# Differential attention: another order of SyncE's transfers in a turn, and the normed output transposed one unit earlier into the other half of a PSUM bank

## The chip, the core and the metric

The kernel runs on one core of a Trainium2 chip. Its engines work side by side, each through its own list of instructions: TensorE (PE, with its weight loads as PEld), VectorE (DVE), ScalarE (ACT), GpSimd (POOL) and SyncE (SP), which here only issues DMAs. They wait for each other through semaphores. The metric is the time of one execution on the device in microseconds; less is better.

## The reference

The whole reference is a stack of two layers on x of shape 16 x 256 x 128: a mixture of experts, a differential attention, the mixture of experts again, a quantized feed-forward, a linear attention and the feed-forward once more. The change touches the differential attention alone:

```
q = (x @ Wq.T + bq)   16 heads, two maps of 8 numbers each; k alike; v: 16 heads of 8
q1, q2, k1, k2 = rope(...)                       # on both maps
a1 = softmax(causal(q1 @ k1.T * 8**-0.5))        # 256 x 256 for each head
a2 = softmax(causal(q2 @ k2.T * 8**-0.5))
out = (a1 - lam * a2) @ v
out = out * rsqrt(mean(out * out) + 1e-6) * head_norm_w * 0.8
return out @ Wo.T + bo                           # added to x
```

The input of the attention is the layernorm of x, and x is first completed with the fetched outputs of the experts.

## The kernel before

`diff_attention` takes the 16 sequences (batches, `NB = 16`) through a pipeline that is four batches deep. The loop `turns` runs 19 turns on every engine. In turn `it`, batch A = `it` is projected, rotated and packed; B = `it - 1` gets its scores and the maxima of their rows (`scores` on PE, `maxima` on DVE); C = `it - 2` gets its transposed scores, its exponentials on ACT and the product with v; D = `it - 3` is divided, normed, multiplied by Wo and added to x. For each engine a turn is a list of 24 units (`STEPS = 24`, variable `u`), written out by hand: what belongs to unit 13 is issued after what belongs to unit 12, and so on. There is no scheduler; the order on each engine is the order in the code.

What the change touches:

- **SyncE's turn** (`turn` under `@block.sync`). It has helpers, each a wait or two and four DMAs (one for `yg`): `block_queries(b, half)` (L1775) copies half of the packed, transposed queries `qT` into the stacked tile `q_block`; `pair_keys` (L1785) does that for the keys; `peaks(b, half)` (L1793) writes the transposed row maxima into a row of `qT`; `spread_values` (L1766) copies `v_raw` into `v_new`; the fetch (L1811) brings 256 KB of expert outputs for a later batch from HBM into `yg`. SyncE waits in order, so a helper that is not ready holds everything behind it.
- **Who needs them.** `scores(B, 0)`, the first score product of the next turn, waits on PE for `q_block_in[0]` (its first instruction is the mask product L2363). `scores_T(C, 0)` (L2384, L2388) stands ahead of it and needs `peaks` and `pair_keys` of the same half. The second halves are needed at unit 12. `v_new` is read by POOL's `keep_v` at unit 3 of the next turn, and `yg` by POOL's `weigh_fetched` at unit 1.
- **The bank of the values.** `m_ps[:, 0]` is one PSUM bank of 512 fp32 columns. At unit 12 PE writes the projected values of A into its columns 0 to 255; at unit 13 ACT copies them to `v_raw` (L1985). At unit 14 PE transposes the normed output of D (`on`, made by DVE at unit 12, L2304; it shares its memory with `osq`, and the profile prints it as `diff_osq`) into the same columns (L2549), and therefore waits for `v_taken`; ACT copies the result to `onT` (L1991). At unit 15 PE transposes the packed queries into this bank (L2573), for which `onT` must have been copied, and ACT's `keep_peaks` (L1948) at unit 15 is what SyncE's `peaks` waits for.

Of the kernel before, what the change touches and what calls it, by code (L numbers as in the profile page):

```python
# [12 lines left out]
ACT = mybir.ActivationFunctionType  # L13
AX = mybir.AxisListType

P = 128
# [1496 lines left out]
def diff_attention(nc, tag, x, ident, neghalf, made, later, ew, routed):  # L1513
# [16 lines left out]
    S = 2 * P  # L1530
    NB = (x.shape[1] - TG) // 2
# [28 lines left out]
    with ExitStack() as ctx:  # L1560
# [54 lines left out]
        on = osq  # L1615
        onT = nm.sb("onT", [P, S], F32)
# [4 lines left out]
        m_ps = nm.ps("m_ps", [P, 2, 512], F32)  # L1621
        m16 = [m_ps[:, i].bitcast(F16) for i in range(2)]

        if ew:
            yg = nm.sb("yg", [P, 2, 2, P], F32)
# [21 lines left out]
        fetched = nm.sem("fetched")  # L1647
        fetch_weighed = nm.sem("fetch_weighed")
        fetch_added = nm.sem("fetch_added")
# [20 lines left out]
        v_taken = nm.sem("v_taken")  # L1670
# [19 lines left out]
        o_weighted = nm.sem("o_weighted")  # L1690
# [6 lines left out]
        onT_in_psum = nm.sem("onT_in_psum")  # L1697
        onT_ready = nm.sem("onT_ready")
# [53 lines left out]
        @block.sync  # L1752
        def _(sp):
            sp.wait_ge(packs_ready, 7)

            def chunks(half):
                return slice(CH // 2 * half, CH // 2 * half + CH // 2)

            def spread_values(b):

                sp.wait_ge(v_taken, b + 1)
                if b >= 1:
                    sp.wait_ge(v_ready, b)
                for i in range(2):
                    for j in range(2):
                        sp.dma_start(v_new[KB * j:KB * j + KB, i::2], v_raw[KB * i:KB * i + KB]).then_inc(v_dup_in, 16)  # L1766

            def block_queries(b, half):

                sp.wait_ge(packT_ready, b * 4 + (4 if half else 1))  # L1770
                if b >= 1:
                    sp.wait_ge(s_ready, (b - 1) * STEPS + HALF * (half + 1))
                for r in range(4):
                    rows = slice(PACK * r, PACK * r + PACK)
                    sp.dma_start(q_block[rows, chunks(half), :, r], qT[rows, b % 3, chunks(half)].rearrange(  # L1775
                        "p c (i q) -> p c i q", q=QB)).then_inc(q_block_in[half], 16)

            def pair_keys(b, half):

                sp.wait_ge(packT_ready, b * 4 + 3)  # L1780
                if b >= 1:
                    sp.wait_ge(st_ready, (b - 1) * EXPS + EXP_HALF * (half + 1))
                for r in range(4):
                    rows = slice(PACK * r, PACK * r + PACK)
                    sp.dma_start(k_pair[rows, r // 2, chunks(half), :, r % 2], kT[rows, b % 2, chunks(half)].rearrange(  # L1785
                        "p c (i k) -> p c i k", k=KB)).then_inc(k_pair_in[half], 16)

            def peaks(b, half):

                sp.wait_ge(peakT_ready, b * 2 + half + 1)  # L1790
                for r in range(4):
                    row = PACK * r + USED - 1
                    sp.dma_start(qT[row:row + 1, b % 3, chunks(half)].rearrange("p c (i q) -> p (c i) q", q=QB),  # L1793
                                 peakT[half][:, QB * r:QB * r + QB].unsqueeze(1)).then_inc(peaks_in[half], 16)

            def turn(A, B, C, D, par):
                if B is not None:
                    block_queries(B, 1)
                if C is not None:
                    pair_keys(C, 1)  # L1800
                    peaks(C, 1)
                if B is not None:
                    pair_keys(B, 0)
                    peaks(B, 0)
                if A is not None:
                    spread_values(A)
                    block_queries(A, 0)
                    if ew and A + 2 < NB:
                        if A >= 1:
                            sp.wait_ge(fetch_added, A * 2)  # L1810
                        sp.dma_start(yg[:], ew.results[:, 2 * A + 4:2 * A + 6]).then_inc(fetched, 16)  # L1811

            turns(sp, turn)
            for half in range(2):
                sp.wait_ge(q_block_in[half], NB * 64)
                sp.wait_ge(k_pair_in[half], NB * 64)
                sp.wait_ge(peaks_in[half], NB * 64)
            sp.wait_ge(v_dup_in, NB * 64)
            if routed:
                for i in range(2):  # L1820
                    sp.wait_ge(scattered[i], len(range(i, routed - 1, 2)) * 2 * TG * 16)
# [99 lines left out]
        def _(a):  # L1921
# [28 lines left out]
            def turn(A, B, C, D, par):  # L1950
                norms, routes, places, sends = groups(D)
                for u in range(STEPS):
# [27 lines left out]
                    if A is not None:  # L1980
                        if u == 13:
                            a.wait_ge(v_in_psum, A + 1)
                            if B is not None:
                                a.wait_ge(v_dup_in, (B + 1) * 64)
                            nc.scalar.activation(v_raw[:].rearrange("p j h d -> p (j h d)"), m_ps[:, 0, 0:S], ACT.Copy).then_inc(v_taken, 1)  # L1985
                    if D is not None:
                        if u == 8:
                            guess_rms(D)
                        if u == 14:
                            a.wait_ge(onT_in_psum, D + 1)  # L1990
                            nc.scalar.activation(onT[:], m_ps[:, 0, 0:S], ACT.Copy).then_inc(onT_ready, 1)  # L1991
                    if B is not None and u == 15:
                        keep_peaks(B, 0)
                    if A is not None:
# [11 lines left out]
                        if u in (11, 12):  # L2006
                            j = u - 11
# [9 lines left out]
                        if u in (17, 18):  # L2017
                            j = u - 17
# [8 lines left out]
                        if u in (21, 22):  # L2027
                            j = u - 21
# [317 lines left out]
        def _(pe):  # L2346
# [110 lines left out]
            def turn(A, B, C, D, par):  # L2457
                norms, routes, places, sends = groups(D)
                for u in range(STEPS):
# [20 lines left out]
                    if u == 1 and A is not None:  # L2480
# [3 lines left out]
                        for j in range(2):  # L2484
                            last = nc.tensor.transpose(m_ps[:, 0, j * P:(j + 1) * P], xn[:, j], ident[:])
# [13 lines left out]
                    if u == 5 and D is not None:  # L2499
# [14 lines left out]
                        for j in range(2):  # L2514
                            for c in range(4):
                                at = (c % 2) * S + j * P
                                last = nc.tensor.transpose(m_ps[:, j, c * P:(c + 1) * P], oT[:, c // 2, at:at + P], ident[:])
                        last.then_inc(o_in_psum, 1)
                    if u == 7 and A is not None:
# [7 lines left out]
                        for j in range(2):  # L2527
                            for part in range(2):
                                last = project(m_ps[:, part, j * QK:(j + 1) * QK], j, slice(part * QK, (part + 1) * QK))
                        last.then_inc(qk_in_psum, 1)  # L2530
                    if u == 12 and A is not None:
                        pe.wait_ge(rope_taken, A * 2 + 2)
                        for j in range(2):
                            last = project(m_ps[:, 0, j * P:(j + 1) * P], j, slice(2 * QK, QKV))
                        last.then_inc(v_in_psum, 1)
                    if routes is not None and u == 13:
# [2 lines left out]
                            router_product(routes)  # L2539
                        else:  # L2540
                            ranks(routes)
                    if u == 14 and D is not None:
                        pe.wait_ge(on_ready, D + 1)
                        if A is not None:
                            pe.wait_ge(v_taken, A + 1)
                        else:
                            pe.wait_ge(o_weighted, D + 1)
                        for j in range(2):
                            last = nc.tensor.transpose(m_ps[:, 0, j * P:(j + 1) * P], on[:, j].rearrange("p h d -> p (h d)"), ident[:])  # L2549
                        last.then_inc(onT_in_psum, 1)  # L2550
                    if u == 15 and B is not None:
                        if routes is not None:
# [24 lines left out]
                    if u == 16 and D is not None:  # L2577
# [9 lines left out]
                        for j in range(2):  # L2587
                            out = m_ps[:, 1, j * P:(j + 1) * P]
                            nc.tensor.matmul(out, two_ones[:], wo_rows[:], start=True, stop=False)
                            last = nc.tensor.matmul(out, onT[:, j * P:(j + 1) * P], wo[:], start=False, stop=True)  # L2590
# [536 lines left out]
```

## Time and profile before

| | |
|---|---|
| median of 3 runs | 1248.44 us (1246.51 to 1251.01) |
| the profiled execution | 1243.69 us, its span 1241.9 us, so 1.8 us lie around the span |
| differential attention | about 239.9 to 779.9 us of the span |
| a full turn (first score product to the next turn's first) | 29 to 33 us |
| granted TensorE clock | 0.92 over the span, 0.95 in the attention |

The profile is that of one execution. A timeline row gives the start, the duration, the engine, the line of the code, the operation with the tile written and the tiles read, how many instructions were merged, and in square brackets how long the engine had been idle before it and what it had waited for. A window row gives busy time and number of instructions, then the granted clock as a share of 2.4 GHz, the DMA engines' busy share and GB/s. "SPq" is SyncE's queue; the duration there is that of issuing the transfers, not of moving the data.

### The profile page before, as it was taken

To read this page: it belongs to the slowest core of one execution; us is meant where nothing else is said; L and a number is where in the kernel's file an instruction comes from. 1 tells how busy PE (TensorE), PEld (TensorE's weight loads), DVE (VectorE), ACT (ScalarE), POOL (GpSimd) and SP (SyncE) were. 2 spreads that over 40 slices of the span, in tenths; PEclk is the share of its full clock that TensorE was granted. 3 is DMA by queue.
4 is the path that set the end of the run, shared out by engine and by line. 5 is a ranking of instruction groups with operands and counts; after the bars stand their busy time and mean duration, and the time that the engine had idled before them with its cause. 6 is when DMAs were issued, how large, how long until landed. Compare 5 with 4: busy or idle time off the path is not lost. (4 is left out here: it accounts for less than half of the span.)

```text
span 1241.9 us, 30962 instructions
## 1 busy us (share of the span) xinstructions
PE 989.9 (80%) x10944; PEld 731.5 (59%) x10976; DVE 859.7 (69%) x2352; ACT 660.6 (53%) x1247; POOL 654.9 (53%) x705
## 2 busy tenths in 40 slices
PE   3762999378888888788888887689993989999597
PEld 1531777145666666565666664578871855666476
DVE  7881887465667776767676765598876937877672
ACT  4730655435666666666656665346652644443163
POOL 5874677243333354544454433517772408888651
PEclk9875999688999999999989999689995989999899
DMA  8213431034433334433444331333314000000001
GB/s 241 80 48 98 116 110 66 34 45 60 54 54 53 56 57 62 58 59 54 61 62 62 51 63 28 110 112 104 99 57 141 3 1 2 1 1 2 1 26 44
DMA packets 273893, 75.52 MB, mean 61 GB/s; under 512 B 217040, under 2 KB 267504, under 8 KB 273360
## 3 DMA queue, kind: packets, MB, share of 16 engines
q1 hardware_dynamic: 264304, 52.51, 22.8%
q0 software_dynamic: 9440, 21.02, 4.9%
q8 instruction: 93, 1.52, 0.6%
q14 instruction: 56, 0.46, 0.1%
HBM read 28.08 MB, written 24.17 MB: 42 GB/s over the span
## 5 line engine op out<-in xcount | busy, mean ns | idle before, releaser
L2111 DVE TENSOR_REDUCE diff_peak<-diff_s_ps 128x2 f16<-128x384 f32 (+7 forms) x384 | 208.4, 558 | 141.1 <-PE diff_s_ps L2366 139.8
L1959 ACT ACTIVATE diff_prob<-diff_st_ps 128x512 f32<-128x512 f32 x320 | 187.1, 598 | 131.3 <-PE diff_st_ps L2388 130.1
L433 POOL DMA_INDIRECT exp_ys<-moe_y_sb,moe_dest x156 | 152.2, 975 | 87.0 <-ACT moe_y_sb L516 53.7
L2388 PE MATMUL diff_st_ps<-diff_qT,diff_k_pair 128*128 128x256 f16 (+3 forms) x1024 | 129.4, 240 | 3.5 <-issue 2.5
L2366 PE MATMUL diff_s_ps<-diff_kT,diff_q_block 128*128 128x32 f16 (+7 forms) x1024 | 130.4, 233 | 0.0
L2404 PE MATMUL diff_ot_ps<-diff_prob,diff_v 128*32 128x256 f32 (+3 forms) x2048 | 112.8, 317 | 0.5 <-ACT diff_prob L1959 0.5
L2363 PE MATMUL diff_s_ps<-diff_mask,diff_ident_bf 128*128 128x64 bf16 (+1 forms) x384 | 81.0, 211 | 39.6 <-DMA diff_q_block<-diff_qT 32.5
L509 ACT ACTIVATE moe_h_hi<-moe_h 128x512 f16<-128x512 f32 x94 | 59.2, 630 | 88.2 <-DVE moe_h L741 88.2
L2718 POOL TENSOR_TENSOR lin_y<-lin_state,lin_qT 128x512 f32<-128x512 f32 x64 | 81.1, 1268 | 15.5 <-DVE lin_state L2866 12.8
L2866 DVE TENSOR_TENSOR_SCAN lin_state<-lin_lam_ps,lin_kv 128x512 f32<-128x512 f32 x64 | 76.6, 1215 | 10.0 <-POOL lin_kv L2705 7.8
L2937 PEld LDWEIGHTS lin_o_ps<-last_lin_wo,lin_y 128*128 128x128 f32 x512 | 65.0, 191 | 26.6 <-POOL lin_y L2718 21.3
L503 ACT ACTIVATE moe_act<-moe_g_ps 128x512 f32<-128x512 f32 x94 | 55.7, 593 | 46.0 <-PE moe_g_ps L963 42.5
L416 POOL DMA_INDIRECT exp_xs<-moe_xh,exp_rows x64 | 66.7, 1042 | 23.8 <-issue 19.0
L2937 PE MATMUL lin_o_ps<-last_lin_wo,lin_y 128*128 128x128 f32 x512 | 70.3, 281 | 10.4 <-POOL lin_y L2718 10.4
L2363 PEld LDWEIGHTS diff_s_ps<-diff_mask,diff_ident_bf 128*128 128x128 bf16 x384 | 38.8, 101 | 61.8 <-issue 39.4
L741 DVE TENSOR_TENSOR moe_h<-moe_act,moe_u_ps 128x512 f32<-128x512 f32 x94 | 64.4, 685 | 15.4 <-PE moe_u_ps L963 14.4
L2388 PEld LDWEIGHTS diff_st_ps<-diff_qT,diff_k_pair 128*128 128x128 f16 x1024 | 70.6, 100 | 5.4
L736 DVE TENSOR_TENSOR moe_h_lo<-moe_h,moe_h_hi 128x512 f16<-128x512 f32 x94 | 65.0, 691 | 10.4 <-ACT moe_h_hi L509 10.0
L2404 PEld LDWEIGHTS diff_ot_ps<-diff_prob,diff_v 128*32 128x32 f32 x2048 | 53.2, 114 | 29.2 <-issue 14.2
L2384 PE MATMUL diff_st_ps<-diff_mask_T,diff_ident_bf 128*128 128x128 bf16 (+1 forms) x288 | 67.9, 236 | 2.0 <-ACT diff_prob L1959 1.8
L2366 PEld LDWEIGHTS diff_s_ps<-diff_kT,diff_q_block 128*128 128x128 f16 x1024 | 66.5, 103 | 3.1 <-issue 0.6
L1016 PE MATMUL moe_o_ps<-exp_down_hi,moe_h_hi 128*128 x312 | 61.4, 220 | 0.8 <-DVE moe_h_lo L736 0.8
(403 smaller groups left out, 2903.8 us busy)
## 6 DMA issues: line engine op xcount, KB each, us to landing
moe_xg<-exp_xs SPq DMA_DIRECT2D x78, 130.0 KB, 2.2
diff_q_block<-diff_qT SPq DMA_DIRECT2D x128, 64.0 KB, 3.4
diff_k_pair<-diff_kT SPq DMA_DIRECT2D x128, 64.0 KB, 2.3
diff_v_new<-diff_v_raw SPq DMA_DIRECT2D x64, 64.0 KB
diff_yg<-exp_ys SPq DMA_DIRECT2D x14, 256.0 KB, 3.6
fetched_yg<-exp_ys SPq DMA_DIRECT2D x7, 512.0 KB, 4.1
exp_ys<-moe_y_sb,moe_dest POOLq DMA_INDIRECT x156, 2.4
all_x<-in_x SPq DMA_DIRECT2D x4, 512.0 KB, 5.0
```

Source lines behind the costliest of these rows:

```text
L416: nc.gpsimd.indirect_dma_start(out=ew.xs, out_offset=bass.IndirectOffsetOnAxis(ap=rows[:, k, t:t + 1], axis=0), in_=xh_of(g)[:, t - g * TG ...
L433: nc.gpsimd.indirect_dma_start(out=ew.ys, out_offset=bass.IndirectOffsetOnAxis(ap=dest[:, s, j:j + 1], axis=0), in_=y_sb[:, s % YR, j], in ...
L1959: nc.scalar.activation(prob[:, n % RING], st_ps[:, e % 2], ACT.Exp, scale=SCALE).then_inc(exp_ready, 1)
L2111: nc.vector.tensor_reduce(peak[:, half, c0:c0 + n, i], s_ps[:, u % 2, 0:n * wd].rearrange("p (c k) -> p c k", k=wd), op=ALU.max, axis=AX.X ...
L2363: nc.tensor.matmul(out[:, :, wd - QB:], ident_bf[:], mask[:, 0:n], start=True, stop=False, skip_group_check=True)
L2366: last = nc.tensor.matmul(out[:, c], q_block[:, ch, i].rearrange("p r q -> p (r q)"), kT[:, B % 2, ch, 0:wd], start=False, stop=True, skip ...
L2384: nc.tensor.matmul(cols, ident_bf[:], mask_T[:, 0:len(equal)], start=True, stop=False, skip_group_check=True)
L2388: last = nc.tensor.matmul(out[:, at:at + wd], k_pair[:, h % 2, h // 2, i].rearrange("p r k -> p (r k)"), qT[:, C % 3, h // 2, KB * i:S], s ...
L2404: last = nc.tensor.matmul(ot_ps[32 * r:32 * r + 32, half, col:col + wd], v[:, b % 2, i, h], prob[:, (b * EXPS + n) % RING, at:at + wd], st ...
L2718: nc.gpsimd.tensor_tensor(y[:, f % RING], state[:, f % STATES], qT[:, b], ALU.mult).then_inc(y_ready, 1)
L2866: nc.vector.tensor_tensor_scan(state[:, f % STATES], lam_ps[:, b], kv[:, f % RING], 0.0, ALU.mult, ALU.add).then_inc(state_ready, 1)
L2937: last = nc.tensor.matmul(o_ps[:, b, t * P:(t + 1) * P], y[:, f % RING, t * P:(t + 1) * P], wo[:, f], start=(f == 0 and t == 0), stop=(f = ...
```

## The change

Two edits. SyncE's turn is now, from the first keys on: `pair_keys(B, 0)`, the fetch of `yg` (with its wait), `peaks(B, 0)`, `block_queries(A, 0)`, `spread_values(A)`. No DMA is added or removed. And PE transposes `on` at unit 13, into columns 256 to 511 of `m_ps[:, 0]`; PE then no longer waits for `v_taken` there, but ACT waits for that transposition ahead of its copy to `v_raw`, and copies `onT` from the new columns at unit 14 as before.

```
--- before.py
+++ after.py
@@ -1801,14 +1801,15 @@
                     peaks(C, 1)
                 if B is not None:
                     pair_keys(B, 0)
+                if A is not None and ew and A + 2 < NB:
+                    if A >= 1:
+                        sp.wait_ge(fetch_added, A * 2)
+                    sp.dma_start(yg[:], ew.results[:, 2 * A + 4:2 * A + 6]).then_inc(fetched, 16)
+                if B is not None:
                     peaks(B, 0)
                 if A is not None:
+                    block_queries(A, 0)
                     spread_values(A)
-                    block_queries(A, 0)
-                    if ew and A + 2 < NB:
-                        if A >= 1:
-                            sp.wait_ge(fetch_added, A * 2)
-                        sp.dma_start(yg[:], ew.results[:, 2 * A + 4:2 * A + 6]).then_inc(fetched, 16)
 
             turns(sp, turn)
             for half in range(2):
@@ -1980,6 +1981,8 @@
                     if A is not None:
                         if u == 13:
                             a.wait_ge(v_in_psum, A + 1)
+                            if D is not None:
+                                a.wait_ge(onT_in_psum, D + 1)
                             if B is not None:
                                 a.wait_ge(v_dup_in, (B + 1) * 64)
                             nc.scalar.activation(v_raw[:].rearrange("p j h d -> p (j h d)"), m_ps[:, 0, 0:S], ACT.Copy).then_inc(v_taken, 1)
@@ -1988,7 +1991,7 @@
                             guess_rms(D)
                         if u == 14:
                             a.wait_ge(onT_in_psum, D + 1)
-                            nc.scalar.activation(onT[:], m_ps[:, 0, 0:S], ACT.Copy).then_inc(onT_ready, 1)
+                            nc.scalar.activation(onT[:], m_ps[:, 0, S:2 * S], ACT.Copy).then_inc(onT_ready, 1)
                     if B is not None and u == 15:
                         keep_peaks(B, 0)
                     if A is not None:
@@ -2539,14 +2542,10 @@
                             router_product(routes)
                         else:
                             ranks(routes)
-                    if u == 14 and D is not None:
+                    if u == 13 and D is not None:
                         pe.wait_ge(on_ready, D + 1)
-                        if A is not None:
-                            pe.wait_ge(v_taken, A + 1)
-                        else:
-                            pe.wait_ge(o_weighted, D + 1)
                         for j in range(2):
-                            last = nc.tensor.transpose(m_ps[:, 0, j * P:(j + 1) * P], on[:, j].rearrange("p h d -> p (h d)"), ident[:])
+                            last = nc.tensor.transpose(m_ps[:, 0, S + j * P:S + (j + 1) * P], on[:, j].rearrange("p h d -> p (h d)"), ident[:])
                         last.then_inc(onT_in_psum, 1)
                     if u == 15 and B is not None:
                         if routes is not None:
```

SyncE's list in a middle turn, before, from the first half of the keys of one turn to the second half of the maxima in the next (`k_pair` is `pair_keys`, `diff_qT<-diff_peakT` is `peaks`, `v_new` is `spread_values`, `yg` the fetch):

```order
L1785 DMA diff_k_pair<-diff_kT 32x16x64 x4
L1793 DMA diff_qT<-diff_peakT 1x32x32 x4
L1766 DMA diff_v_new<-diff_v_raw 64x2x128 x4
L1775 DMA diff_q_block<-diff_qT 32x32x32 x4
L1811 DMA diff_yg<-exp_ys 128x2x256
L1775 DMA diff_q_block<-diff_qT 32x32x32 x4
L1785 DMA diff_k_pair<-diff_kT 32x16x64 x4
L1793 DMA diff_qT<-diff_peakT 1x32x32 x4
```

And the same stretch of the changed kernel:

```order
L1785 DMA diff_k_pair<-diff_kT 32x16x64 x4
L1807 DMA diff_yg<-exp_ys 128x2x256
L1793 DMA diff_qT<-diff_peakT 1x32x32 x4
L1775 DMA diff_q_block<-diff_qT 32x32x32 x4
L1766 DMA diff_v_new<-diff_v_raw 64x2x128 x4
L1775 DMA diff_q_block<-diff_qT 32x32x32 x4
L1785 DMA diff_k_pair<-diff_kT 32x16x64 x4
L1793 DMA diff_qT<-diff_peakT 1x32x32 x4
```

The fetch moved up past the maxima, the queries and the values, and the queries' first half moved up past the values; the second half of the queries has the values in front of it where the fetch was.

PE's list around units 13 to 15 of a turn that also routes tokens, before (`exp_router` rows are the router product of unit 13, `diff_st_ps` the transposed scores, `diff_s_ps` the scores, `diff_osq` the normed output, `diff_peak` the maxima, `diff_q_pack` the packed queries):

```order
L2429 MATMUL diff_m_ps<-exp_router_hi,exp_xT 128x8
L2384 MATMUL diff_st_ps<-diff_mask_T,diff_ident_bf 128x2x64
L2388 MATMUL diff_st_ps<-diff_qT,diff_k_pair 128x256 x2
L2363 MATMUL diff_s_ps<-diff_mask,diff_ident_bf 128x4x32
L2366 MATMUL diff_s_ps<-diff_kT,diff_q_block 128x96 x4
L2549 MATMUL diff_m_ps<-all_ident,diff_osq 128x128 x2
L2384 MATMUL diff_st_ps<-diff_mask_T,diff_ident_bf 128x2x64
L2388 MATMUL diff_st_ps<-diff_qT,diff_k_pair 128x256 x2
L2363 MATMUL diff_s_ps<-diff_mask,diff_ident_bf 128x4x32
L2366 MATMUL diff_s_ps<-diff_kT,diff_q_block 128x128 x4
L2445 MATMUL diff_m_ps<-diff_ident_h,diff_peak 32x128
L2573 MATMUL diff_m_ps<-diff_ident_h,diff_q_pack 128x128 x8
```

And the same stretch of the changed kernel:

```order
L2432 MATMUL diff_m_ps<-exp_router_hi,exp_xT 128x8
L2548 MATMUL diff_m_ps<-all_ident,diff_osq 128x128 x2
L2387 MATMUL diff_st_ps<-diff_mask_T,diff_ident_bf 128x2x64
L2391 MATMUL diff_st_ps<-diff_qT,diff_k_pair 128x256 x2
L2366 MATMUL diff_s_ps<-diff_mask,diff_ident_bf 128x4x32
L2369 MATMUL diff_s_ps<-diff_kT,diff_q_block 128x96 x4
L2387 MATMUL diff_st_ps<-diff_mask_T,diff_ident_bf 128x2x64
L2391 MATMUL diff_st_ps<-diff_qT,diff_k_pair 128x256 x2
L2366 MATMUL diff_s_ps<-diff_mask,diff_ident_bf 128x4x32
L2369 MATMUL diff_s_ps<-diff_kT,diff_q_block 128x128 x4
L2448 MATMUL diff_m_ps<-diff_ident_h,diff_peak 32x128
L2572 MATMUL diff_m_ps<-diff_ident_h,diff_q_pack 128x128 x8
```

The two transpositions of `on` moved ahead of the transposed scores and the scores of unit 14; everything else stands as it stood. ACT's and DVE's lists have the same order as before.

## Rows read from the trace of the kernel before

**Rows 1.** Window of the attention: us, PE, PEld, DVE, ACT, POOL busy (x), PEclk, DMA share, GB/s

```profile
239.90:779.90 540.00, 443.06 (x6249) 324.09 (x6280) 371.34 (x986) 332.60 (x621) 234.05 (x306) 0.95 0.36 54
```

**Rows 2.** The list of waits: engine, line, waited for, total us, times, longest

```profile
PE diff_s_ps L2363 <- DMA diff_q_block<-diff_qT: 32.5, 16, 4.0
...
PE diff_m_ps L2549 <- ACT diff_v_raw L1985: 16.7, 13, 1.4
```

**Rows 3.** Timeline of SyncE's queue, 511 to 541 us

```profile
512.71 2.66 SPq L1785 DMA_DIRECT2D diff_k_pair<-diff_kT  x4
520.58 3.13 SPq L1793 DMA_DIRECT2D diff_qT<-diff_peakT  x4
523.81 2.67 SPq L1766 DMA_DIRECT2D diff_v_new<-diff_v_raw  x4
526.58 2.95 SPq L1775 DMA_DIRECT2D diff_q_block<-diff_qT  x4
529.58 0.77 SPq L1811 DMA_DIRECT2D diff_yg<-exp_ys  x1
531.16 3.30 SPq L1775 DMA_DIRECT2D diff_q_block<-diff_qT  x4
...
537.90 2.52 SPq L1793 DMA_DIRECT2D diff_qT<-diff_peakT  x4
```

**Rows 4.** Timeline of PE at the end of that turn

```profile
529.96 0.38 PE L2388 MATMUL diff_st_ps<-diff_qT,diff_k_pair 128*128 128x256 f16 x2
532.38 0.22 PE L2363 MATMUL diff_s_ps<-diff_mask,diff_ident_bf 128*128 128x128 bf16 x1 [2.04 <-DMA diff_q_block<-diff_qT]
```

**Rows 5.** Timelines of ACT (units 16 and 23) and DVE, same turn

```profile
521.55 1.02 ACT L2025 ACTIVATE diff_qT<-diff_m_ps 128x1024 f16<-128x1024 f16 x1
...
530.11 1.02 ACT L2025 ACTIVATE diff_qT<-diff_m_ps 128x1024 f16<-128x1024 f16 x1 [0.71 <-PE diff_m_ps L2573]
...
532.73 0.30 DVE L2111 TENSOR_REDUCE diff_peak<-diff_s_ps 128x4 f16<-128x128 f32 x1 [3.11 <-PE diff_s_ps L2366]
```

**Rows 6.** Views of line L1775, then of line L1793: landing of their transfers

```profile
DMA to landing us min/median/max: 2.6/3.4/4.2
...
DMA to landing us min/median/max: 1.7/1.8/3.6
```

**Rows 7.** Windows of two whole turns: us, PE busy (x), PEclk, DMA share, GB/s

```profile
500.44:532.38 31.94, 25.61 (x381) 1.00 0.43 63
...
564.19:597.39 33.20, 26.86 (x381) 0.95 0.37 55
```

**Rows 8.** Timeline of PE at the end of the second of these turns

```profile
597.39 0.22 PE L2363 MATMUL diff_s_ps<-diff_mask,diff_ident_bf 128*128 128x128 bf16 x1 [2.78 <-DMA diff_q_block<-diff_qT]
```

**Rows 9.** Timeline of ACT, units 12 to 15 of the turn from 500.44

```profile
517.33 0.63 ACT L2016 ACTIVATE diff_q_pack<-diff_by_cos 128x512 f16<-128x512 f32 x1 [1.09 <-POOL diff_by_cos L1901]
...
518.34 0.38 ACT L1985 ACTIVATE diff_v_raw<-diff_m_ps 128x256 f32<-128x256 f32 x1
518.61 0.60 ACT L1959 ACTIVATE diff_prob<-diff_st_ps 128x512 f32<-128x512 f32 x1
...
519.56 0.41 ACT L1991 ACTIVATE diff_onT<-diff_m_ps 128x256 f32<-128x256 f32 x1
...
520.30 0.26 ACT L1948 ACTIVATE diff_peakT<-diff_m_ps 32x128 f16<-32x128 f16 x1
```

**Rows 10.** Timelines of DVE and PE, units 12 to 15 of that turn

```profile
516.67 0.91 DVE L2304 TENSOR_TENSOR diff_osq<-diff_o,diff_rms 128x256 f32<-128x256 f32 x1
...
516.80 0.22 PE L2384 MATMUL diff_st_ps<-diff_mask_T,diff_ident_bf 128*128 128x128 bf16 x1
518.86 0.41 PE L2549 MATMUL diff_m_ps<-all_ident,diff_osq 128*128 128x128 f32 x2 [1.40 <-ACT diff_v_raw L1985]
...
520.11 0.61 PE L2573 MATMUL diff_m_ps<-diff_ident_h,diff_q_pack 128*128 128x128 f16 x8
```

**Rows 11.** Timeline of PE, unit 12 of that turn

```profile
514.41 0.22 PE L2384 MATMUL diff_st_ps<-diff_mask_T,diff_ident_bf 128*128 128x128 bf16 x1
```

More of the change, by code:

```diff
@@ L1803, in turn @@
                     pair_keys(B, 0)
+                if A is not None and ew and A + 2 < NB:
+                    if A >= 1:
+                        sp.wait_ge(fetch_added, A * 2)
+                    sp.dma_start(yg[:], ew.results[:, 2 * A + 4:2 * A + 6]).then_inc(fetched, 16)
+                if B is not None:
                     peaks(B, 0)
                 if A is not None:
+                    block_queries(A, 0)
                     spread_values(A)
[L1807 to L1811, printed above, removed]
             turns(sp, turn)
@@ L1982, in turn @@
                             a.wait_ge(v_in_psum, A + 1)
+                            if D is not None:
+                                a.wait_ge(onT_in_psum, D + 1)
                             if B is not None:
@@ L1990, in turn @@
                             a.wait_ge(onT_in_psum, D + 1)
-                            nc.scalar.activation(onT[:], m_ps[:, 0, 0:S], ACT.Copy).then_inc(onT_ready, 1)
+                            nc.scalar.activation(onT[:], m_ps[:, 0, S:2 * S], ACT.Copy).then_inc(onT_ready, 1)
                     if B is not None and u == 15:
@@ L2541, in turn @@
                             ranks(routes)
-                    if u == 14 and D is not None:
+                    if u == 13 and D is not None:
                         pe.wait_ge(on_ready, D + 1)
[L2544 to L2547, printed above, removed]
                         for j in range(2):
-                            last = nc.tensor.transpose(m_ps[:, 0, j * P:(j + 1) * P], on[:, j].rearrange("p h d -> p (h d)"), ident[:])
+                            last = nc.tensor.transpose(m_ps[:, 0, S + j * P:S + (j + 1) * P], on[:, j].rearrange("p h d -> p (h d)"), ident[:])
                         last.then_inc(onT_in_psum, 1)
```

## The prediction

> **What bounds the kernel now.** I start with the window over the attention: in 540.0 us PE is busy for 443.1, DVE for 371.3, ACT for 332.6 and POOL for 234.1 [rows 1]. PE is the fullest engine, but it stands idle for about 97 us, so the next question is what ends its idle times. The list of waits names two that the change touches: the first score product of a turn waits for the stacked queries' DMA, 32.5 us in 16 waits, the longest 4.0; and the transposition of the normed output waits for ACT's copy of the values, 16.7 us in 13 waits, 1.4 at most [rows 2]. A wait in that list is worth its length only if nothing else would end at the same place, so I read each in the timelines.
>
> Take the turn that ends at 532.38. SyncE issues, back to back, the maxima from 520.58 (3.13 us), the values from 523.81 (2.67), the first half of the queries from 526.58 (2.95) and the fetch from 529.58 (0.77) [rows 3]. PE has issued its last product at 529.96 and then starts L2363 at 532.38, after 2.04 us idle, so it was ready at 530.34 [rows 4]. DVE has waited 3.11 us for that product, and ACT's last copy of the turn ends at 531.13 [rows 5]. So at this point nobody works on the path that the next turn needs, except the queue. In this turn the whole pipeline stands still for a DMA that was issued behind four others which are not needed before unit 3 of the next turn.
>
> **The change, part by part.** *The queries go ahead of the values.* The copy of `qT` that the queries need ends at 521.55 + 1.02 = 522.57 [rows 5], before SyncE is through with the maxima at 523.71. So in the new order the queries take the place of the values and are issued from 523.81 instead of 526.58, 2.77 us earlier. I assume that what follows (issue time, and the landing 2.6 to 4.2 us after it [rows 6]) is the same. The last of them lands at about 532.38 - 2.77 = 529.61, 0.73 us before PE is ready. The wait is then gone in this turn. Over all turns: the list has 16 waits with 32.5 us; the longest, 4.0, keeps 4.0 - 2.8 = 1.2; the other 28.5 us can go except for a hand-over, which I read as 0.14 us between the end of the values' copy at 518.72 and PE's start at 518.86 [rows 9, 10]: 15 x 0.1 = 1.5 us left. Gain 32.5 - 1.2 - 1.5 = 29.8 us. Bounds of this term: nothing, if another wait of the same length takes its place (rivals), and 32.5.
>
> *The values go behind the queries.* They are issued 3 us later. POOL reads them at unit 3 of the next turn and makes of them what PE uses a whole turn later, so a turn of some 30 us covers this; without that cover it would cost up to 3 us a turn.
>
> *The fetch goes up* into SyncE's pause between the keys (issued until 512.71 + 2.66 = 515.37) and the maxima (520.58): 5.2 us for an issue of 0.8 [rows 3]. What it waits for is POOL's addition at unit 7, and the keys ahead of it are released only at unit 9, so it waits for nothing. At the end of the turn it no longer stands in front of the second half of the queries. These start at 531.16 only because ACT's copy ends at 531.13 [rows 3, 5], so I count nothing.
>
> *The transposition one unit earlier.* PE waited 1.40 us in unit 14 in this turn, which looks like 16.7 us to be had. The timelines say otherwise. ACT works without a gap from 517.33 (released by POOL) to 520.56: queries, exponentials, `v_raw` at 518.34, `onT` at 519.56, `keep_peaks` at 520.30 [rows 9]. The next thing that matters on PE, the transposition of the packed queries at 520.11, needs the `onT` copy that ends at 519.97, and SyncE's maxima need `keep_peaks`. Neither depends on when PE had transposed `on`, as long as it is there by 519.56. In the new order DVE delivers `on` at 516.67 + 0.91 = 517.58; PE, ready at 516.80, waits until about 517.72, transposes for 0.41 and is done at 518.13 [rows 10]. ACT may then take the values at 518.27, and did so at 518.34: 0.07 us to spare. The transposed scores of unit 14 follow at 518.0 instead of 516.80 and are needed at 518.61 [rows 9]; they fit with about 0.2 us. PE then has the 1.4 us wait in two smaller pieces, before unit 14 and in unit 15 before 520.11. I count 0. Bounds: it gains 16.7 us if I misread the chain, and costs 0.9 us a turn (518.86 - 1.40 - 516.80 is the part that PE used before and now waits, rounded up), 15 us, if none of it is covered. For the range I use 0.3 us a turn either way, 5 us, because the margins just named are of that size.
>
> *The clock.* Two turns of the same work: 31.94 us at a granted clock of 1.00 and 33.20 at 0.95 [rows 7]. Without the closing waits of 2.04 and 2.78 [rows 4, 8] they are 29.90 and 30.42, so a turn at 0.95, which contains a stretch at 1.2 GHz instead of 2.4, costs 0.5 us. The mean over the attention is 0.95 [rows 1], which for 16 turns is 8 us at most. PE's longest pauses are the ones removed; I take 3 us, with 0 and 8 as bounds.
>
> **Sum.** 1243.69 (the profiled execution: span 1241.9 and 1.8 around it) - 29.8 - 3 + 0 = 1210.9 us. The median of the runs shown is 4.75 above that execution, so I forecast 1248.44 - 32.8 = 1215.6, rounded 1216.
>
> **A rule against it.** SyncE's four issues for the values take 2.67 us, and one transfer of the queries lands 3.4 us after its issue [rows 3, 6]: here four issues are about as long as a transfer. The Trainium skill, "DMA: Bandwidth & Descriptors", section "Issuing engines are not separate DMA queues", calls the time to initiate a DMA "usually small relative to the DMA itself". By that rule the place in the queue would be worth little and the time would stay near 1248; by the rows it is 2.77 us a turn. I follow the rows.
>
> **Rivals.**
> *Another wait takes part of the place* (0.14). The second halves of keys and maxima start behind ACT's copy as before, while PE's turn begins 2 us earlier. The maxima are issued until 540.42, 8.04 us after the turn's start [rows 3]; that becomes 10.1, and landing after 1.8 (at most 3.6 [rows 6]) gives 11.9 to 13.7. PE asks for them at 514.41, 13.97 us after 500.44 [rows 11]. It fits, by 0.3 to 2 us. If this or a wait for ACT or DVE early in the turn gives back 1 us a turn, the gain is 33 - 16 = 17 us: 1231.
> *More than the sum* (0.05): the clock gives back all 8 us and the transposition some: below 1207.
> *The wait is bandwidth, not order* (0.05). If the queries' transfers land when the DMA engines are through with everything, an earlier issue gives nothing: 1248. Against it: a mean DMA share of 0.43 in this turn [rows 7], and a landing that follows the issue by at most 4.2 us.
> *Slower* (0.04). ACT's copy of the values now waits for DVE's `on` through PE, and behind it stand the exponentials, `onT` and `keep_peaks`, which release PE, the maxima and the queries. `on` could come late, since it takes 0.91 us at a place where POOL works too. Each us that it is late beyond 0.07 is a us of the turn. It decides from about 2 us a turn (33 / 16); at 3 us it would be 1216 + 48 = 1264. Nothing in the rows is late by so much.
>
> **Chances and range.** The forecast, 1207 to 1224, has 0.72. What a measurement here can tell from no change is about 0.3%, 4 us. Faster by more than that: 0.72 + 0.14 + 0.05 = 0.91; within it 0.05; slower 0.04. The range runs from 1207 (the clock's and the transposition's bounds) to 1234 (the partial rival), and leaves out the upper part of that rival, no gain, slower, and the lowest case.
>
> **What the profile after should show.** PE's wait for the queries' DMA at L2366 (formerly L2363) falls from 32.5 to under 4 us in total, with one of about 1.2 left; the queries are issued directly behind the maxima; turns last 29 to 30.5 us; the attention takes about 507 us instead of 540; PE's wait for the values' copy is gone, in its place waits for DVE's `on` (0.9 us) and for the `onT` copy; ACT's row from `q_pack` to `keep_peaks` stays without a gap; the clock in the attention is above 0.95. The prediction is wrong if the first score product still waits over 1 us a turn, if a wait at unit 12 appears, or if ACT waits for the transposition at unit 13.

## The result and the profile after

The changed kernel takes 1201.69 us (median of 4 runs, 1199.37 to 1203.58) against 1248.92 us; the ratio is 0.962, with a 95% interval of 0.959 to 0.965. That is 47 us less, where 33 us were forecast, and it lies below the forecast range. The direction and the mechanism were right; the size of one term, the clock's, was not.

The profiled execution of the changed kernel has a span of 1198.0 us, 43.9 us less than that of before. The difference between 43.9 and 47 is that each profiled execution stands at another distance from its median, so I explain the 43.9 (the execution before is 5.2 us faster than its median, the one after 1.9).

First the queue. Timeline of SyncE, the same stretch of a turn as in [rows 3]:

```profile
500.71 3.21 SPq L1793 DMA_DIRECT2D diff_qT<-diff_peakT  x4
504.02 2.79 SPq L1775 DMA_DIRECT2D diff_q_block<-diff_qT  x4
506.91 3.31 SPq L1766 DMA_DIRECT2D diff_v_new<-diff_v_raw  x4
511.29 3.56 SPq L1775 DMA_DIRECT2D diff_q_block<-diff_qT  x4
514.94 2.65 SPq L1785 DMA_DIRECT2D diff_k_pair<-diff_kT  x4
517.63 3.40 SPq L1793 DMA_DIRECT2D diff_qT<-diff_peakT  x4
```

The queries are issued directly behind the maxima, as expected, and the values follow while PE finishes the turn. Timeline of PE at the turn's end, which answers to [rows 4]:

```profile
509.58 0.62 PE L2572 MATMUL diff_m_ps<-diff_ident_h,diff_q_pack 128*128 128x128 f16 x8 [0.57 <-ACT diff_kT L2037]
510.04 0.22 PE L2387 MATMUL diff_st_ps<-diff_mask_T,diff_ident_bf 128*128 128x128 bf16 x1
510.09 0.38 PE L2391 MATMUL diff_st_ps<-diff_qT,diff_k_pair 128*128 128x256 f16 x2
510.31 0.22 PE L2366 MATMUL diff_s_ps<-diff_mask,diff_ident_bf 128*128 128x128 bf16 x1
```

And of DVE at the same place, which answers to [rows 5]:

```profile
510.66 0.30 DVE L2114 TENSOR_REDUCE diff_peak<-diff_s_ps 128x4 f16<-128x128 f32 x1 [0.91 <-PE diff_s_ps L2369]
```

The first score product follows the transposed scores without a wait. DVE waits 0.91 us for its result instead of 3.11, so it is still ready before PE and does not set this place.

What stands in the list of waits now at the places that the prediction spoke of, and the window over the attention:

```profile
PE diff_m_ps L2572 <- ACT diff_kT L2037: 8.8, 14, 1.4
...
PE diff_m_ps L2572 <- ACT diff_onT L1994: 8.6, 13, 0.7
PE diff_m_ps L2548 <- DVE diff_osq L2307: 7.6, 14, 0.7
...
PE diff_s_ps L2366 <- DMA diff_q_block<-diff_qT: 2.9, 3, 1.5
```

```profile
239.90:735.30 495.40, 432.50 (x6276) 313.28 (x6274) 374.47 (x984) 330.65 (x620) 235.02 (x306) 0.98 0.38 59
```

PE's wait for the queries has fallen from 32.5 us to 2.9 us in 3 waits. The 16.7 us of waiting for the values' copy are gone too, but 8.6 and 7.6 us stand in their place; the wait for the copy of the keys, 8.8 us, is an old one (9.4 before). The attention takes about 495 us where it took 540.

Now the surprise. Windows over units 0 to 11 of three turns of the kernel before (us, PE busy (x), PEclk, DMA share, GB/s), then of two turns of the changed one:

```profile
407.76:420.41 12.65, 12.25 (x185) 1.00 0.45 65
532.38:546.42 14.04, 13.70 (x185) 0.88 0.39 51
564.19:579.01 14.82, 13.77 (x181) 0.88 0.40 51
```

```profile
510.31:522.95 12.64, 12.41 (x187) 1.00 0.45 65
538.38:552.58 14.20, 12.64 (x184) 1.00 0.40 57
```

The 185 products of the first two windows are the same work. At a granted clock of 1.00 they took 12.65 us, at 0.88 they took 14.04, and PE's busy time grew by as much as the window (1.45 and 1.39 us). The changed kernel has, in this execution, 1.00 in this place in every turn from the second on, and its five turns of this kind (every second one) all take 12.64 us up to unit 12. Before, a stretch at 1.2 GHz began in the pause or at most 1.1 us behind it in 11 of the 14 turns from the second on, though not in each: a pause of 2.04 us at 532.38 was followed by one, and the turn from 500.44, after a pause of 2.15 us, was at 1.00 throughout [rows 7].

Over the 15 turns between the first score product of the first and that of the last turn, the time went from 465.6 to 421.0 us. The pauses ahead of the first score product give 32.0 - 1.6 = 30.4 us of these 44.6. Units 0 to 11 give 205.9 - 192.8 = 13.0 us. The rest of the turns gives 1.2 us. Outside these turns the two executions are alike within 1 us.

### The profile page after: what moved, and what is told of

Its sections match the earlier page's. It is cut to its first block and busy times, and to the rows that moved or that the text cites. A ratio compares the mean times of both kernels' runs of the same rounds, so it can differ in the third digit from the quotient of the medians.

```text
span 1198.0 us, 30977 instructions
## 1 busy us (share of the span) xinstructions
PE 974.8 (81%) x10976; PEld 718.8 (60%) x10976; DVE 863.2 (72%) x2352; ACT 659.2 (55%) x1247; POOL 656.8 (55%) x705
## 5 line engine op out<-in xcount | busy, mean ns | idle before, releaser
L2369 PE MATMUL diff_s_ps<-diff_kT,diff_q_block 128*128 128x32 f16 (+7 forms) x1024 | 127.5, 228 | 0.0
L2391 PE MATMUL diff_st_ps<-diff_qT,diff_k_pair 128*128 128x256 f16 (+3 forms) x1024 | 122.9, 233 | 0.0
L2407 PE MATMUL diff_ot_ps<-diff_prob,diff_v 128*32 128x256 f32 (+3 forms) x2048 | 109.3, 307 | 0.5 <-ACT diff_prob L1960 0.5
L2387 PE MATMUL diff_st_ps<-diff_mask_T,diff_ident_bf 128*128 128x128 bf16 (+1 forms) x320 | 78.2, 244 | 1.8 <-ACT diff_prob L1960 1.2
L2391 PEld LDWEIGHTS diff_st_ps<-diff_qT,diff_k_pair 128*128 128x128 f16 x1024 | 68.2, 98 | 4.7
L2407 PEld LDWEIGHTS diff_ot_ps<-diff_prob,diff_v 128*32 128x32 f32 x2048 | 50.7, 108 | 28.8 <-issue 13.5
L2369 PEld LDWEIGHTS diff_s_ps<-diff_kT,diff_q_block 128*128 128x128 f16 x1024 | 63.2, 99 | 3.1 <-issue 1.6
L1892 POOL TENSOR_TENSOR diff_k_pack<-diff_by_cos,diff_k_pack 128x256 f16<-128x256 f32 x32 | 21.6, 679 | 71.8 <-ACT diff_k_pack L2024 71.6
```

The source lines that it names most:

```text
L2369: last = nc.tensor.matmul(out[:, c], q_block[:, ch, i].rearrange("p r q -> p (r q)"), kT[:, B % 2, ch, 0:wd], start=False, stop=True, skip ...
L2387: nc.tensor.matmul(cols, ident_bf[:], mask_T[:, 0:len(equal)], start=True, stop=False, skip_group_check=True)
L2391: last = nc.tensor.matmul(out[:, at:at + wd], k_pair[:, h % 2, h // 2, i].rearrange("p r k -> p (r k)"), qT[:, C % 3, h // 2, KB * i:S], s ...
L2407: last = nc.tensor.matmul(ot_ps[32 * r:32 * r + 32, half, col:col + wd], v[:, b % 2, i, h], prob[:, (b * EXPS + n) % RING, at:at + wd], st ...
```

## The experiments

All ratios are to the kernel before, measured on the same chip as the kernel in question. The theories: **A, the clock**: the 14 us beyond the pauses come from TensorE not falling to 1.2 GHz any more; **B**: they are the transposition's; **C**: they come from the fetch, which went up in the queue and no longer keeps POOL and the DMA engines busy at the turn's start.

### SyncE's order alone, and the transposition alone

The first kernel leaves the transposition where it was (the hunks of ACT and PE are undone), the second leaves SyncE's turn as it was (the first hunk is undone).

> SyncE's new order alone; the transposition of the normed output stays in unit 14 and in the values' columns. Theory A (clock): of the 47 us that the change gained, about 30 are the removed waits for the queries and about 14 come from TensorE no longer falling to 1.2 GHz after them; the transposition gives nothing. Then this kernel is as fast as the changed one, ratio to before 0.962, and no stretch of lower clock between 300 and 700 us. Rival B (transposition): the 14 us are the transposition's; ratio 0.974. Rival C (less traffic and less waiting of POOL, because the fetch went up): 0.962 too, told apart by the third kernel.

Measured: 1203.34 us, ratio 0.9635 (0.9617 to 0.9652). No wait for the queries is left that counts (1.7 us over the 15 turns), and the clock from 300 to 700 us is 1.00.

> The transposition at unit 13 into the other half of the bank alone; SyncE's order as before. Theory A: ratio 1.000 (within 0.002), the wait for the queries' DMA stays at about 32 us, and TensorE waits in unit 15 for the copy to onT instead of in unit 14. Rival B: 0.989. A loss through ACT's new wait would show as above 1.002.

Measured: 1246.07 us, ratio 0.9976 (0.9951 to 1.0001). The waits moved as expected:

```profile
PE diff_s_ps L2365 <- DMA diff_q_block<-diff_qT: 29.9, 14, 4.2
...
PE diff_m_ps L2571 <- ACT diff_onT L1993: 8.7, 13, 0.7
PE diff_m_ps L2547 <- DVE diff_osq L2306: 7.5, 14, 0.7
```

The 16.7 us of [rows 2] have become 8.7 + 7.5 = 16.2 us of other waits, and the clock from 300 to 700 us is 0.96. B has fallen: the order alone brings all of the gain that these runs can see. Whether the transposition is worth 0.2% by itself they do not decide (two of its 12 runs took 1235 and 1236 us, the others 1243 to 1252), so it was measured again on top of the order.

### On one chip: the changed kernel and the order alone, again

> The changed kernel as it is, once more, on the chip that also runs the next two. The reference point for them: ratio to before 0.962.

> SyncE's new order without the transposition's move, on the same chip. If the transposition is worth nothing, this ratio is within 0.002 of the one of the changed kernel; the transposition alone, on the kernel before, had given 0.9976 with an interval that reaches 1.000, and if that 0.2% is real this one is 0.964 to 0.965.

On this chip the kernels take some 10% longer (before 1368.12 us), so only the ratios are compared. Changed: 1326.42 us, 0.9696 (0.9667 to 0.9724). Order alone: 1326.77 us, 0.9696 (0.9666 to 0.9726). The transposition's move is worth nothing that these runs can see. The gain is 41.7 us on this chip instead of 47, and the ratio that had been expected for the changed kernel, 0.962, lies outside the interval; there is no profile of the kernel before from this chip, so where the missing 5 us are stays open. In the profile of the changed kernel its 15 turns take 426.7 us instead of 421.0; the extra time lies ahead of the attention (its first score product is at 310.7 us instead of 261.6) and behind it (583 instead of 515 us), where the experts and the other layers are computed. Most of the 5.7 us in the turns are one turn, from 645.97, which took 33.6 us. It had no pause ahead of its first score product, but PE waited inside it for DVE:

```profile
650.57 0.69 PE L2488 MATMUL diff_m_ps<-all_ident,diff_xn 128*128 128x128 f32 x2 [2.35 <-DVE diff_xn L2319]
```

A stretch of 6.8 us at 1.2 GHz began in this wait. So the lower clock is not tied to the wait for the queries.

### Which part of the order

Only the two helpers swapped, with the fetch last as before:

```
                 if A is not None:
-                    spread_values(A)
                     block_queries(A, 0)
+                    spread_values(A)
                     if ew and A + 2 < NB:
```

> Only the two helpers swapped: queries ahead of the values; the fetch stays last, the transposition as before. Theory A: the wait goes and with it the lower clock: ratio 0.962 to 0.966 (the fetch and the values in front of the second half of the queries are hidden until unit 12). Rival C: the fetch at the turn's end costs what it cost before: about 0.974. Rival B: 0.974 as well.

Measured: 1206.62 us, ratio 0.9656 (0.9633 to 0.9679). The 15 turns take 424.4 us, pauses 2.9 us, clock 1.00.

Only the fetch moved up, the values still ahead of the queries:

```
                 if B is not None:
                     pair_keys(B, 0)
+                if A is not None and ew and A + 2 < NB:
+                    ...
+                    sp.dma_start(yg[:], ...).then_inc(fetched, 16)
+                if B is not None:
                     peaks(B, 0)
                 if A is not None:
                     spread_values(A)
                     block_queries(A, 0)
```

> The kernel before with the fetch moved up alone; values still ahead of the queries. The queries are issued no earlier, so by theory A (the gain is the pause before the first score product and the lower clock that follows it) the wait stays near 32 us and the ratio is 1.000, at best 0.997. By rival C (the fetch's traffic and POOL's wait for it carry 10 us or more) it is 0.99.

Measured: 1248.86 us, ratio 0.9992 (0.9971 to 1.0014). The pauses are 33.5 us and units 0 to 11 take 204.9 us, as before, at a clock of 0.95. C has fallen: the fetch alone moves nothing. About nine tenths of the gain (0.0344 of 0.0378) are four issues that changed places with four others. The tenth that is left (0.9656 against 0.9635 with the fetch moved up too) is within the intervals and not shown.

### The pause filled

The kernel before, with dummy products ahead of PE's wait for the queries. They go to the free score bank and change no output.

```
                 if not (below(B, 1) and u < 2):
                     pe.wait_ge(max_ready, B * STEPS + u - 1)
                 ...
+                if u == 0 and B >= 1:
+                    for i in range(8):
+                        nc.tensor.matmul(s_ps[:, 0], ew.ident_h[:], ew.up_hi[:, 0]..., start=True, stop=True)
                 if k == 0:
                     pe.wait_ge(q_block_in[half], B * 64 + 64)
```

> The kernel before, with 8 dummy products of 512 columns (each about 0.22 us at full clock, 1.7 us in all) issued by TensorE into the free score bank ahead of its wait for the queries in each of 15 turns; they add nothing to the output. The wait for the queries is nearly filled but not shortened. Theory A: TensorE keeps the full clock through the turn's start, so about 13 us are gained though nothing is issued earlier: ratio 0.988 to 0.992, full clock from 300 to 700 us. Rivals B and C: no gain, 1.000, or a few us lost where the products outlast the wait.

Measured: 1242.22 us, ratio 0.9956 (0.9933 to 0.9979). The gain is half of what A expected. Window over units 0 to 11 of two turns, of the same kind as that from 532.38 in the kernel before:

```profile
532.71:545.37 12.66, 12.43 (x187) 1.00 0.43 62
594.66:607.32 12.66, 12.42 (x186) 1.00 0.46 64
```

Nothing was issued earlier, and yet these units take 12.66 us instead of 14.04. Rivals B and C have no explanation for that. Over the 15 turns units 0 to 11 fell from 205.9 to 199.6 us, 6.3 and not 13: the first two turns and two of the last four kept stretches at 1.2 GHz, and in the turn from 437.63, at full clock, PE waited 2.4 us inside these units for DVE's `xn`. The dummies outlasted the wait in some turns; all else in the turns is 1.6 us longer, which I put down to that.

The same with 4 dummies (`range(4)`):

> The kernel before with 4 dummy products (0.9 us) instead of 8 ahead of the wait for the queries; they add nothing to the output. With 8 the first 12 units of the odd turns took 12.65 us instead of 13.7 to 14.1, but in some turns the dummies outlasted the wait. With 4 they never do. Theory A: if the pause's length decides the clock, most of the 47.5 us of lower clock go and the ratio is 0.990; if it needs less idleness than 4 products give, part of them stays and it is 0.995. Rivals: 1.000.

Measured: 1243.44 us, ratio 0.9956 (0.9933 to 0.9978), near the lesser of A's two figures: of the 47.5 us at the lower clock, 18.2 stay. In the profile units 0 to 11 take 197.1 us together, and the window of the turn at this place is

```profile
531.43:544.08 12.65, 12.42 (x185) 1.00 0.41 55
```

So 0.9 us of work in a pause of 2 us was enough in this turn too. In another a pause of 2.58 us remained in spite of them and 6.8 us at the lower clock followed; units 0 to 11 of that turn took 15.9 us. In a third 1.86 us remained and 3.4 us followed.

### The pause put back

The changed kernel, but PE also waits for the values ahead of the first score product:

```
+                if u == 0 and B >= 1:
+                    pe.wait_ge(v_dup_in, (B + 1) * 64)
                 if k == 0:
                     pe.wait_ge(q_block_in[half], B * 64 + 64)
```

> The changed kernel, all of it, but TensorE waits ahead of the first score product of a turn for the values' landing too (they land some 2.8 us after the queries). Fetch, queries and transposition stay where the change put them; only the pause is back. Theory A: the pause brings the lower clock back with it; 30 us and 10 to 14 us return, ratio 0.995 to 1.000, 30 to 50 us of lower clock in the attention. Rival B or C: only 30 us return, ratio 0.987, and the first 12 units of an odd turn still take 12.6 us.

Measured: 1230.51 us, ratio 0.9849 (0.9820 to 0.9877). A's ratio, 0.995 to 1.000, did not come; 0.985 is near the 0.987 that B and C had named, but for another reason. They have 30 us of pauses and nothing else; what came is 20.5 us of pauses and 7.9 us in units 0 to 11. The pause came back only in part, because the values land sooner than I had counted: 1.7 us after their last issue ended (588.72 to 590.42), where the queries in [rows 3, 4] took 2.85 us.

```profile
PE diff_s_ps L2368 <- DMA diff_v_new<-diff_v_raw: 20.1, 13, 4.0
```

Against the profile of the changed kernel the 15 turns are 29.6 us longer: 20.5 us of pauses, 7.9 us in units 0 to 11, 1.2 us elsewhere. Windows over units 0 to 11 of two turns of the same kind in this one execution:

```profile
528.02:540.65 12.63, 12.40 (x185) 1.00 0.40 51
590.42:604.42 14.00, 13.81 (x185) 0.88 0.36 45
```

The same 185 products, in the same program, with the same queue: 12.63 us at a clock of 1.00, 14.00 at 0.88. PE is busy 1.41 us longer in the second and idle for as little as in the first (0.19 and 0.23 us), so it is the products themselves that take longer. The pause ahead of the second was 2.08 us:

```profile
590.42 0.22 PE L2368 MATMUL diff_s_ps<-diff_mask,diff_ident_bf 128*128 128x128 bf16 x1 [2.08 <-DMA diff_v_new<-diff_v_raw]
```

Ahead of the first it was 1.38 us. B and C were right about four of the five turns of this kind: after pauses of 0.57 to 1.38 us they still took 12.64 us, and this one alone took 14.00. Over the 15 turns 34.2 us were at the lower clock, where the changed kernel has 9.2.

Here a us of pause went with 0.4 us more in units 0 to 11 (7.9 / 20.5), and in the change it was the same share (13.0 / 30.4 = 0.43).

### A faster version

In the changed kernel PE still waits 0.57 us in unit 23, for ACT's copy of the second half of the keys (the row at 509.58 above), because the packed queries go to the bank that this copy reads. With the two banks of the keys swapped, it is the first half's copy that matters:

```
-    last = nc.tensor.transpose(m16[1 - j][:, c * P:(c + 1) * P], ...)      # PE, units 20 and 21
+    last = nc.tensor.transpose(m16[j][:, c * P:(c + 1) * P], ...)
...
-    pe.wait_ge(packT_ready, A * 4 + 3)                                     # PE, unit 23
+    pe.wait_ge(packT_ready, A * 4 + 2)
...
-    pe.wait_ge(packT_ready, B * 4 + 2)                                     # PE, unit 0, peaks_T(C, 1)
+    pe.wait_ge(packT_ready, B * 4 + 3)
```

ACT reads `m16[j]` accordingly, and the wait for `x_added` moves from `j == 0` to `j == 1`.

> The changed kernel with the two PSUM banks of the key transpositions swapped: the first half of the keys goes to the bank of the queries, so that the second half of the queries (unit 23) waits for the first key copy of ACT instead of the second. In the changed kernel that wait is 0.57 us of idle TensorE in a turn, 15 times, and it ends the turn. If TensorE sets the turn's length there, 15 x 0.6 = 9 us are gained, ratio to before 0.955; if ACT's copies behind it set it (they are 1 us each), nothing, 0.962.

Measured: 1197.47 us, ratio 0.9589 (0.9563 to 0.9615). Timeline of PE at the turn's end:

```profile
505.26 0.61 PE L2572 MATMUL diff_m_ps<-diff_ident_h,diff_q_pack 128*128 128x128 f16 x8
505.71 0.22 PE L2387 MATMUL diff_st_ps<-diff_mask_T,diff_ident_bf 128*128 128x128 bf16 x1
505.77 0.38 PE L2391 MATMUL diff_st_ps<-diff_qT,diff_k_pair 128*128 128x256 f16 x2
505.98 0.22 PE L2366 MATMUL diff_s_ps<-diff_mask,diff_ident_bf 128*128 128x128 bf16 x1
```

The wait of unit 23 is gone, and the 15 turns take 416.0 us instead of 421.0, where 9 us had been hoped for. The waits for the queries rise from 2.9 to 5.9 us in the list of waits, since PE now is sometimes ready before they land, and units 0 to 11 take 195.6 us together instead of 192.8.

> The swapped banks of the keys on top of SyncE's new order, without the transposition's move. The same comparison for the faster kernel: 0.959 if the transposition is worth nothing, 0.961 if it is worth 0.2%. With the 0.57 us wait of unit 23 shortened by the swap in either case, it should be 0.3% below the order-only kernel.

Measured, on the slower chip: 1319.74 us, ratio 0.9653 (0.9620 to 0.9686), against 0.9696 with the order alone on that chip. The swap gains 0.3% on top of the changed kernel (0.9589 against 0.962) and 0.4% here, but the intervals of the kernels with and without it overlap both times, so the gain is likely and not certain.

## Why the prediction was right or wrong

**The queries ahead of the values: right.** 29.8 us were predicted, 30.4 are measured over the 15 turns (29.6 by the list of waits, which has the first turn's wait too). The longest wait kept 1.46 us where 1.2 were counted. The 0.1 us of hand-over that I left for the other waits did not appear.

**The clock: this is the step that failed.** The prediction says: "so a turn at 0.95 [...] costs 0.5 us", and "I take 3 us, with 0 and 8 as bounds". The measured share is the 13.0 us of units 0 to 11, of which about 11 are the clock's by the following estimate. In the turns of one kind the first 12 units take 12.64 us at full clock in both kernels, so all of their loss is the clock's. In the others, two turns at full clock before the change took 14.3 us and those after it 13.6 to 14.2, so up to half a us a turn may be something else; it sums to about 2 us. PE is busy for 12.3 to 12.6 us in all of these and differs in how long it waits, mostly for DVE; why it waited longer before, the experiments do not resolve.

Two things went wrong. The pair of turns that I compared was of the second kind, where VectorE has 43 instructions in these units instead of 25 and PE waits for it. There the lower clock is partly hidden: PE was busy 1.25 us longer (12.52 and 13.77 in units 0 to 11), but idle 0.75 us less (1.80 and 1.05), which leaves the 0.5 us. The turn from 532.38, which begins where the turn that I read closely ends, is of the first kind, and there the same stretch costs 14.04 - 12.65 = 1.4 us. The turn that shows this, from 407.76, was in the trace. And the bound of 8 us was not a bound, since it multiplied that one price by the number of turns. I then took less than half of it without a reason from a row. The rule should have been to price both kinds of turn.

The 10 us that this term lacked are most of what the forecast missed: the profiles differ by 43.9 us and not 32.8, which is 10.0 for this term, 0.6 for the pauses and 0.5 for all else. The other 3.3 us between 43.9 and 47.2 are the distances of the two executions from their medians, which no term could foresee.

**Which case came.** It was the rival "more than the sum", to which I gave 0.05, and by its first half alone: the clock. The lower end of the range rested on the same price (and by its own terms it is 1216 - 5 - 5 = 1206, not 1207).

**The transposition: right at 0.** The two new waits are there, 8.6 us for the `onT` copy and 7.6 us for DVE, and the same kernel with and without the move gives 0.9696 twice. The prediction's bound of 0.9 us a turn was too high by its own numbers, 518.86 - 1.40 - 516.80 = 0.66; nothing rested on it. ACT's chain is what it was. Timeline of ACT in the changed kernel, units 12 to 15, which answers to [rows 9]:

```profile
497.46 0.63 ACT L2019 ACTIVATE diff_q_pack<-diff_by_cos 128x512 f16<-128x512 f32 x1 [1.09 <-POOL diff_by_cos L1902]
498.00 0.58 ACT L1960 ACTIVATE diff_prob<-diff_st_ps 128x512 f32<-128x512 f32 x1
498.47 0.38 ACT L1988 ACTIVATE diff_v_raw<-diff_m_ps 128x256 f32<-128x256 f32 x1
...
499.69 0.41 ACT L1994 ACTIVATE diff_onT<-diff_m_ps 128x256 f32<-128x256 f32 x1
...
500.43 0.25 ACT L1949 ACTIVATE diff_peakT<-diff_m_ps 32x128 f16<-32x128 f16 x1
```

From `q_pack` to the start of `keep_peaks` it is 2.97 us, as before (517.33 to 520.30). Timeline of PE there:

```profile
497.76 0.44 PE L2548 MATMUL diff_m_ps<-all_ident,diff_osq 128*128 128x128 f32 x2 [0.67 <-DVE diff_osq L2307]
...
500.24 0.61 PE L2572 MATMUL diff_m_ps<-diff_ident_h,diff_q_pack 128*128 128x128 f16 x8 [0.73 <-ACT diff_onT L1994]
```

The transposition ends at 498.20, and ACT takes the values at 498.47, 1.01 us after the start of `q_pack`, as before (517.33 to 518.34): the margin held.

**The fetch and the values: right at 0**, the first shown by itself, the second not by itself. POOL now waits 24.5 us in 11 waits for the values, as the list of waits has it, and yet the turns of the first kind take 12.64 us up to unit 12 as they did before at full clock.

**The signs.** None of the three signs of being wrong came. But the turns last 28.1 to 29.7 us from 366 us on where 29 to 30.5 were expected, and the attention 495 where 507 were: both mostly by the clock's term again.

**The rule against the change** (the Trainium skill, "DMA: Bandwidth & Descriptors", "Issuing engines are not separate DMA queues": the time to initiate a DMA is usually small relative to the DMA itself): for a single DMA the traces agree, since one issue of the queries took about 0.7 us and its landing came 3.4 us after it [rows 6]. What the prediction said would follow from it, a place in the queue that is worth little, did not come. Four issues in a row take 2.7 to 3.6 us in the first timeline above, about as long as a landing, and four issues that changed places with four others were worth 41 us (1247.92 to 1206.62), the clock included.

## What to carry to other kernels

- In a queue that waits in order, put the transfers in the order in which their readers need them, and count the issue time: four small transfers took about 3 us of the queue here.
- A pause of TensorE may cost more than its length. Look at the granted clock of the stretch behind it, and price it separately for every kind of iteration, by pairs with the same number of instructions: what it costs where another engine is the bound says little about where TensorE is.
- A wait that has another one right behind it was worth nothing here. Follow the chain to the next instruction that others wait for before you count it.

## What was not expected of the hardware

- Whether a pause of about 2 us was followed by a stretch at 1.2 GHz differed from turn to turn: it was after 1.44, 2.04 and 2.08 us, and it was not after 2.15 or, in the kernel with the transposition alone, after 2.31. One also began in a wait of 2.35 us for DVE inside a turn, and none came with another such wait of 2.43 us. With 0.9 us of dummy products in it, it mostly was not. Where it came, the window of 12.6 us showed a clock of 0.88 and 1.4 us more.
- The kernel before took 1249 us on one chip and 1368 us on another. For the changed kernel, which was profiled on both, 117 of the 122.5 us between the two spans lie outside the 15 turns of the attention.
